# A two-layer AdaLN transformer on one core: the second division of layer 0's heads, two products sooner in VectorE's and GpSimd's order

## The chip, the cores and the metric

The kernel runs on one core of one Trainium2 chip. The metric is the device time of the whole kernel in microseconds (us), the median of three runs. An engine works through its own list of instructions in order; a semaphore wait stops that engine and nothing else. The engines here are TensorE (PE in the profile, its weight loads PEld), VectorE (DVE), ScalarE (ACT), GpSimd (POOL) and SyncE (SP), which issues the DMAs.

## The reference

Two layers work on `x`, 8 batches of 256 tokens of 128 numbers. Each layer adds a gated attention and a gated feed-forward part, and in front of each stands a layer norm that is scaled and shifted by values from `c`. The change touches layer 0's attention alone, whose 16 heads come down to 4 after the mean over groups:

```python
gq = q.reshape(B, G, KV_HEADS, N, D_HEAD)
gk = k.reshape(B, G, KV_HEADS, N, D_HEAD).mean(axis=1)
gv = v.reshape(B, G, KV_HEADS, N, D_HEAD).mean(axis=1)
scores = jnp.einsum('bghnd,bhsd->bhns', gq, gk) + gbias
attn = jax.nn.softmax(scores, axis=-1)
out = jnp.einsum('bhns,bhsd->bhnd', attn, gv)
```

Layer 0's feed-forward part is a mixture of experts per head: for each token and head one of eight experts is chosen, a causal attention follows, and `einsum('bhne,ehkd,bnhk->...')` goes through the chosen output expert. Layer 1 has an attention over the 16 heads of each token and a feed-forward part with eight experts and a capacity. All is float32.

## The kernel before

The kernel is a software pipeline over the eight batches. A function `in_order` writes down one order of work, and each engine runs `in_order` with its own bodies for the pieces (`attn0`, `values`, `front1`, `products`, ...), so that all engines go through the same places. A piece of work of another batch is put beside a loop: the loop calls `beside(place)`, and a dictionary says which steps come at which place. The order of an engine's instructions is therefore written out by hand, and it is not changed at run time.

`products(b, beside)` is layer 0's output experts for one batch: 16 products, numbered by `c`. VectorE makes mask `c + 7` (L1348: the chosen experts, 8-bit, times `oT`, 128 x 512) and then calls `beside(c)`; TensorE waits for mask `c`, does two matmuls (L1853), and then calls `beside(c)`. Seven masks are ahead when the loop starts, so mask 13 is made at place 6, 14 at 7 and 15 at 8.

Beside these products runs the attention of layer 0 for a later batch, `attn0` (dictionary `in_products0`), with the four heads in two pairs. Its steps are:

- QKV: the projections (TensorE L1662, L1666, L1677) and their copies (ScalarE).
- S0, S1: the logits of a pair of heads (TensorE L1693); VectorE adds the bias and takes the greatest (L1233); ScalarE takes the exponentials with their sums (L811).
- N0, N1: the division of a pair. VectorE waits for the pair's exponentials (semaphore `a_e`) and makes the reciprocal of the sums (L1240); GpSimd waits for this (`a_r`) and multiplies the two heads (L650, 128 x 512 each). TensorE and ScalarE have nothing in these steps.
- T0, T1: TensorE waits for each divided head (`a_pn`) and transposes it, four transposes a head (L1709); ScalarE copies the result (L826, L821).
- V0, V1, OUT: the weighting of the values (TensorE L1720) and the copy out (L829).

For the batches 0 and 1, which run ahead in the opening (20 to 40 us), VectorE divides one head of each pair itself (L1246) and GpSimd the other.

In the rounds in the middle the end of layer 1's attention of an earlier batch lies beside the same products (`in_products`). ADD at place 5 adds to `x` and takes the statistics of the layer norm (VectorE L1216, L1201, L1204), from which GpSimd makes `rstd` (L715 adds epsilon, L717 takes the power). NORM at place 7 is VectorE's: it waits for `rstd` and writes `xn`, two instructions L1211. MODULATE at place 9 transposes `xn` on TensorE (L1635, one transpose for each of the two) and applies the modulation on ScalarE (L774). LOGITS at place 11 (TensorE L2033, VectorE L1472) and PROBS at 13 (L1478) follow. The softmax of layer 1's attention (`softmax`) lies there as well: MAXES at place 9 (VectorE L1405, then GpSimd's subtraction L672), EXPS at 12 and SUMS at 14.

Where several plans have steps at one place, the softmax's come first, then `attn0`'s, then those of layer 1's tail. `attn0` of batches 2 to 7 lies beside products of batches 0 to 5; layer 1's tail lies there from the products of batch 2 on, that is in four of the six.

The two engines' bodies of the division:

```python
if n in (N0, N1):                       # VectorE
    p = (N0, N1).index(n)
    dve.wait_ge(s_("a_e"), b * 8 + 4 * p + 4)
    dve.reciprocal(rdenA[:, 4 * p:4 * p + 4], denA[:, 4 * p:4 * p + 4]).then_inc(s_("a_r"), 1)
if n in (N0, N1):                       # GpSimd
    p = (N0, N1).index(n)
    pool.wait_ge(s_("a_r"), b * 2 + p + 1)
    for h in (2 * p, 2 * p + 1)[:1 if early_batch(b) else 2]:
        pool.tensor_tensor(v, v, rdenA[...], ALU.mult).then_inc(s_("a_pn"), 1)
```

Of the kernel before, what the change touches and what calls it, by code (L numbers as in the profile page):

```python
# [44 lines left out]
TAKE, QKV, S0, S1, N0, N1, T0, T1, V0, V1, OUT = range(10, 21)  # L45
# [15 lines left out]
def adaln_kernel(nc, a, out):  # L61
    with ExitStack() as ctx:
# [318 lines left out]
        def in_order(attn0, values, turns, front1, back1, products, masks, opening, last_softmax, after_attn0, after_products,  # L381
# [8 lines left out]
            def alone(place):  # L390
                pass

            in_products0 = {"start": (QKV,), 1: (S0,), 4: (N0, S1), 7: (T0,), 8: (N1,), 11: (T1,), 14: (V0, V1), 15: (OUT,)}
            in_products = {2: (PROJECT,), 5: (ADD,), 7: (NORM,), 9: (MODULATE,), 11: (LOGITS,), 13: (PROBS,)}
            softmax = {"start": (ADDS,), 9: (MAXES,), 12: (EXPS,), 14: (SUMS,)}
            softmax_behind_masks = {6: (ADDS,), 9: (MAXES,), 12: (EXPS,), 14: (SUMS,)}
# [201 lines left out]
        def _(pool):  # L598
# [120 lines left out]
            def after_attn1(b, k, n):  # L719
                after(b, k, n)  # L720
                if n == LOGITS:
                    pool.wait_ge(s_("n_h"), k + 1 + B)
                    pool.tensor_copy(hE[:, bass.ds(b * N, N)], hR[:, :]).then_inc(s_("h_kept"), 1)

            beside = in_order(attn0, values, nothing, front1, back1, products, nothing, opening, last_softmax, after, after,
                              after_front1, after_attn1)
            for b in range(2):
# [5 lines left out]
        def _(act):  # L733
# [246 lines left out]
            def last_softmax(b, beside):  # L980
# [5 lines left out]
                for i in range(2 * T):  # L986
                    keep(0, i)
                beside("probs")

            beside = in_order(attn0, values, turns, front1, back1, products, nothing, opening, last_softmax, after_attn0,  # L990
                              after_products, after_front1, after_attn1)

# [101 lines left out]
        def _(dve):  # L1094
# [368 lines left out]
            def after_attn1(b, k, n):  # L1463
# [10 lines left out]
                if n == PROBS:  # L1474
# [4 lines left out]
                                      lrec[:, :].unsqueeze(2).broadcast_to([P, T, E1]), ALU.mult).then_inc(s_("l_d"), 1)  # L1479

            beside = in_order(attn0, values, turns, front1, back1, products, masks, opening, last_softmax, after_attn0,
                              after_products, after_front1, after_attn1)
            for b in range(2):
# [725 lines left out]
```

## Time and profile before

| | before |
|---|---|
| time, median of 3 runs (lowest to highest) | 759.81 us (759.73 to 759.92) |
| time of the profiled execution | 759.72 us |
| its span, first to last instruction | 757.8 us |
| TensorE busy | 736.5 us (97%) |
| VectorE busy | 553.4 us (73%) |
| ScalarE busy | 384.9 us (51%) |
| GpSimd busy | 187.6 us (25%) |

The share of busy time is a mean over stages. What one wait is worth is read from the stage in which it stands: from the chain of work that ended last, and from the timelines of the engines, which give each instruction's start and duration and the idle time in front of it.

### The profile page before, as it was taken

To read this page: it belongs to the slowest core of one execution; us is meant where nothing else is said; L and a number is where in the kernel's file an instruction comes from. 1 tells how busy PE (TensorE), PEld (TensorE's weight loads), DVE (VectorE), ACT (ScalarE), POOL (GpSimd) and SP (SyncE) were. 2 spreads that over 40 slices of the span, in tenths; PEclk is the share of its full clock that TensorE was granted. 3 is DMA by queue.
4 is the path that set the end of the run, shared out by engine and by line. 5 is a ranking of instruction groups with operands and counts; after the bars stand their busy time and mean duration, and the time that the engine had idled before them with its cause. 6 is when DMAs were issued, how large, how long until landed. Compare 5 with 4: busy or idle time off the path is not lost.

```text
span 757.8 us, 16811 instructions
## 1 busy us (share of the span) xinstructions
PE 736.5 (97%) x6559; PEld 557.8 (74%) x6559; DVE 553.4 (73%) x1642; ACT 384.9 (51%) x1069; POOL 187.6 (25%) x235
## 2 busy tenths in 40 slices
PE   7899999999999999999999999999999899999996
PEld 5566857775786578657865886688578778999996
DVE  4877785868867886778677867787959664255997
ACT  3755657355545654564456445643561446554422
POOL 0232522154015402530254025304210422000000
PEclk9999999999999999999999999999999999999999
DMA  7950020402040204020402130113204304000000
GB/s 209 398 139 1 29 57 2 112 1 57 13 102 2 57 21 93 2 56 19 97 1 56 28 87 15 43 37 78 57 2 113 112 4 110 1 1 1 16 21 22
DMA packets 55702, 43.07 MB, mean 57 GB/s; under 512 B 37900, under 2 KB 48804, under 8 KB 54216
## 3 DMA queue, kind: packets, MB, share of 16 engines
q1 hardware_dynamic: 55624, 42.01, 20.6%
q8 instruction: 52, 0.85, 0.5%
q14 instruction: 26, 0.21, 0.1%
HBM read 32.42 MB, written 9.58 MB: 55 GB/s over the span
## 4 chain that ended last, share of the span: by engine, by line
PE 81%; DVE 12%; POOL 2%; ACT 2%; issue 2%; DMA 1%; SPq 0%; DVEq 0%; ACTq 0%
PE ps L1770 15%; PE ps L1853 11%; PE ps L1913 8%; PE ps L2076 4%; PE ps L2054 4%; PE ps L1756 4%; PE ps L2023 4%; PE ps L1778 4%; PE ps L1865 3%; PE ps L1804 3%; PE ps L1791 3%; DVE shared L1499 2%; DVE shared L1492 2%; PE ps L1936 2%; PE ps L1948 2%; PE ps L1720 2%
## 5 line engine op out<-in xcount | busy, mean ns | idle before, releaser
L1770 PE MATMUL ps<-veF,hB 128*128 128x512 f32 x256 | 121.6, 606 | 0.0
L1318 DVE COPY_PREDICATED shared<-ghot,ps 128x512 f32<-128x512 int32 x128 | 88.3, 727 | 3.4 <-PE ps L1770 0.6
L865 ACT ACTIVATE sc<-sc,nmax 128x128 f32<-128x128 f32 (+1 forms) x128 | 57.2, 448 | 58.4 <-DVE nmax L1304 58.4
L1770 PEld LDWEIGHTS ps<-veF,hB 128*128 128x128 f32 x256 | 45.2, 189 | 49.4 <-issue 40.5
L658 POOL TENSOR_TENSOR sc<-sc,rg 128x384 f32<-128x384 f32 x64 | 51.7, 829 | 69.9 <-DVE rg L1291 69.9
L715 POOL TENSOR_TENSOR ve<-mv,eps 128x2 f32<-128x2 f32 x24 | 8.6, 358 | 230.5 <-DVE mv L1204 230.5
L1853 PE MATMUL ps<-wide,oeF 128*128 128x256 f32 x256 | 62.3, 386 | 0.0
L1913 PE MATMUL ps<-hC,early 128*64 128x128 f32 x1024 | 61.5, 275 | 0.2
L1853 PE MATMUL ps<-early_masks,oeF 128*128 128x256 f32 x256 | 61.3, 382 | 0.0
L2054 PE MATMUL ps<-hE,veF 128*128 128x256 f32 x256 | 59.5, 382 | 0.3 <-ACT wide L974 0.3
L1913 PEld LDWEIGHTS ps<-hC,early 128*64 128x64 f32 x1024 | 55.6, 137 | 5.2 <-issue 3.0
L650 POOL TENSOR_TENSOR sc<-sc,rdenA 128x512 f32<-128x512 f32 x28 | 28.6, 1041 | 112.6 <-DVE rdenA L1240 112.6
L1853 PEld LDWEIGHTS ps<-wide,oeF 128*128 128x128 f32 x256 | 46.7, 190 | 9.7 <-issue 4.3
L1853 PEld LDWEIGHTS ps<-early_masks,oeF 128*128 128x128 f32 x256 | 47.4, 191 | 7.7 <-issue 2.0
L2054 PEld LDWEIGHTS ps<-hE,veF 128*128 128x128 f32 x256 | 47.1, 190 | 7.0 <-ACT wide L974 0.9
L1348 DVE TENSOR_TENSOR early_masks<-chosen,oT 128x512 f32<-128x512 uint8 x64 | 42.1, 684 | 13.6 <-PE ps L1853 12.7
L811 ACT ACTIVATE sc<-sc,nmax 128x256 f32<-128x256 f32 x64 | 31.7, 498 | 31.0 <-DVE nmax L1233 31.0
L1304 DVE CUSTOM_DVE_ANT_0 sc<-ps,causal 128x128 f32<-128x128 f32 (+1 forms) x128 | 40.0, 350 | 9.5 <-PE ps L1778 9.1
L903 ACT ACTIVATE wide<-ps,bqkvT 128x128 f32<-128x128 f32 x128 | 36.1, 374 | 16.1 <-PE ps L1913 16.0
L1348 DVE TENSOR_TENSOR wide<-chosen,oT 128x512 f32<-128x512 uint8 x64 | 42.1, 695 | 0.5 <-PE ps L1853 0.5
L1387 DVE TENSOR_TENSOR early<-ps,early 128x512 f32<-128x512 f32 x32 | 22.1, 689 | 22.4 <-PE ps L1913 22.1
L672 POOL TENSOR_TENSOR wide<-wide,max 128x512 f32<-128x512 f32 x32 | 32.5, 1044 | 22.5 <-DVE max L1405 22.5
(262 smaller groups left out, 1544.2 us busy)
## 6 DMA issues: line engine op xcount, KB each, us to landing
chosen<-hot_scratch SPq DMA_DIRECT2D x16, 512.0 KB, 5.7
v_scratch<-shared SPq DMA_DIRECT2D x16, 512.0 KB, 5.1
vg<-v_scratch SPq DMA_DIRECT2D x16, 512.0 KB, 5.3
veF<-in_L_ffn_value_experts SPq DMA_DIRECT2D x1, 2048.0 KB, 10.2
oeF<-in_L_ffn_output_experts SPq DMA_DIRECT2D x1, 2048.0 KB, 15.3
early<-in_L_attn_w_qkv SPq DMA_DIRECT2D x1, 1536.0 KB, 15.9
shared<-bias_scratch SPq DMA_DIRECT2D x2, 512.0 KB, 4.9
veF<-in_L_ffn_W SPq DMA_DIRECT2D x1, 1024.0 KB, 5.4
```

The source lines that it names most:

```text
L658: pool.tensor_tensor(v, v, rg[:, h, :].unsqueeze(2).broadcast_to([P, 3, P]), ALU.mult).then_inc(s_("f_pn"), 1)
L672: pool.tensor_tensor(quarter(q), quarter(q), max1[:, q, :].unsqueeze(2).broadcast_to([P, PER_ROUND, ROWS]), ALU.subtract).then_inc(s_("c_s ...
L811: act.activation(v, v, ACT.Exp, bias=nmax[:, h, t:t + 1], scale=-1.0, accum_out=denA[:, h * T + t:h * T + t + 1]).then_inc(s_("a_e"), 1)
L865: act.activation(v, v, ACT.Exp, bias=nmax[:, h % RING, t:t + 1], scale=-1.0, accum_out=denB[:, h * T + t:h * T + t + 1]).then_inc(s_("f_e" ...
L903: act.activation(q1[:, :, 2 * j + i, :], ps[:, qk_bank(b, j), i * P:(i + 1) * P].rearrange("p (n t) -> p n t", t=GT), ACT.Identity, bias=b ...
L1304: dve.tensor_tensor_reduce(sc[:, h % RING, lo:hi], ps[:, 4 + 2 * (h % 2), lo:hi], causal[:, P:N] if t == 0 else causal[:, :], -float(DH) * ...
L1318: dve.copy_predicated(val[:, t, :].rearrange("p (h k) -> p h k", h=HF), ghot[:, t * HF:(t + 1) * HF, e].bitcast(I32).unsqueeze(2) .broadca ...
L1348: dve.tensor_tensor(masked(c), chosen[:, c // 4, 2 * (c % 4):2 * (c % 4) + 2, :], oT[:, c // 4, :].unsqueeze(1).broadcast_to([P, 2, N]), A ...
L1770: pe.matmul(ps[:, vbank(j), :], tok(hB, t), veF[:, :].rearrange("p (h e k) -> p e h k", h=HF, e=EF)[:, e, :, :], start=True, stop=True).th ...
L1853: mm = pe.matmul(ps[:, product_bank(b), 0:N], oeF[:, c // 4, (2 * c + j) % 8, :], masked(c)[:, j, :], start=(c == 0 and j == 0), stop=(c = ...
L1913: mm = pe.matmul(ps[c * DH:(c + 1) * DH, qk_bank(b, j), i * P:(i + 1) * P], wqkv1[:, 4 * quad + i, w, :], tok(hC, c), start=True, stop=True)
L2054: mm = pe.matmul(ps[:, hidden_bank(b, e), g * N:(g + 1) * N], w1[:, e, g * P:(g + 1) * P], hE[:, b * N:(b + 1) * N], start=True, stop=True)
```

## The change

One entry of the dictionary `in_products0` moves: N1, the division of heads 2 and 3, stands at place 6 instead of place 8. All else is the same.

```diff
-            in_products0 = {"start": (QKV,), 1: (S0,), 4: (N0, S1), 7: (T0,), 8: (N1,), 11: (T1,), 14: (V0, V1), 15: (OUT,)}
+            in_products0 = {"start": (QKV,), 1: (S0,), 4: (N0, S1), 6: (N1,), 7: (T0,), 11: (T1,), 14: (V0, V1), 15: (OUT,)}
```

## Rows read from the trace of the kernel before

**Rows 1.** The page: its head, and the chain that ended last by engine.

```profile
span 757.8 us, 16811 instructions
...
PE 81%; DVE 12%; POOL 2%; ACT 2%; issue 2%; DMA 1%; SPq 0%; DVEq 0%; ACTq 0%
```

**Rows 2.** Chain of waits, 205 to 246 us: start, us, what.

```profile
227.63 2.05 POOL sc L650 x2
```

**Rows 3.** Timeline of TensorE, same stretch: start, us, instruction, [idle before <- releaser].

```profile
224.10 1.04 PE L1709 MATMUL ps<-ident,sc 128*128 128x128 f32 x8
224.97 1.89 PE L1853 MATMUL ps<-early_masks,oeF 128*128 128x256 f32 x8
226.70 0.55 PE L1635 MATMUL ps<-ident,xn 128*128 128x128 f32 x2
227.09 1.89 PE L1853 MATMUL ps<-early_masks,oeF 128*128 128x256 f32 x8
228.82 0.60 PE L1709 MATMUL ps<-ident,sc 128*128 128x128 f32 x4
229.73 0.66 PE L1709 MATMUL ps<-ident,sc 128*128 128x128 f32 x4 [0.31 <-POOL sc L650]
230.22 0.51 PE L2033 MATMUL ps<-wg,hA 128*128 128x8 f32 x4
```

**Rows 4.** Timeline of VectorE, same stretch.

```profile
224.35 1.26 DVE L1348 TENSOR_TENSOR wide<-chosen,oT 128x512 f32<-128x512 uint8 x2
226.27 0.60 DVE L1211 TENSOR_SCALAR xn<-x,mv,rstd 128x128 f32<-128x128 f32 x2 [0.65 <-issue]
...
227.38 0.17 DVE L1240 RECIPROCAL rdenA<-denA 128x4 f32<-128x4 f32 x1
227.47 2.43 DVE L1405 TENSOR_REDUCE max<-wide 128x8 f32<-128x512 f32 x4
```

**Rows 5.** Timeline of GpSimd, same stretch.

```profile
224.52 0.55 POOL L715 TENSOR_TENSOR ve<-mv,eps 128x2 f32<-128x2 f32 x1 [2.26 <-DVE mv L1204]
225.15 1.03 POOL L717 TENSOR_TENSOR rstd<-ve,half 128x2 f32<-128x2 f32 x1
227.63 2.04 POOL L650 TENSOR_TENSOR sc<-sc,rdenA 128x512 f32<-128x512 f32 x2 [1.46 <-DVE rdenA L1240]
```

**Rows 6.** Who waited for GpSimd's L650, whole span: us in total, times.

```profile
  PE ps L1709: 1.8, 5
```

**Rows 7.** Timeline of ScalarE, same stretch: last sum of head 3.

```profile
223.66 0.19 ACT L811 ACTIVATION_READ_ACCUMULATOR sc<-sc,nmax 128x1 f32 x1
```

**Rows 8.** Timelines of TensorE and GpSimd, products of batch 1 (138 to 172 us).

```profile
154.79 1.04 PE L1709 MATMUL ps<-ident,sc 128*128 128x128 f32 x8
...
152.03 2.04 POOL L650 TENSOR_TENSOR sc<-sc,rdenA 128x512 f32<-128x512 f32 x2 [2.52 <-DVE rdenA L1240]
```

**Rows 9.** L1211, whole span (ns least/median/most); timeline of all engines, 36 to 38.5 us.

```profile
L1211 DVE TENSOR_SCALAR xn<-x,mv,rstd x48: 323/342/998, 36.9 to 652.1; 128x128 f32<-128x128 f32 x48
...
36.12 0.70 POOL L717 TENSOR_TENSOR rstd<-ve,half 128x2 f32<-128x2 f32 x1
36.78 1.04 POOL L650 TENSOR_TENSOR sc<-sc,rdenA 128x512 f32<-128x512 f32 x1
36.91 1.25 DVE L1211 TENSOR_SCALAR xn<-x,mv,rstd 128x128 f32<-128x128 f32 x2 [0.43 <-issue]
```

**Rows 10.** Timelines of VectorE and GpSimd, later in the first stage.

```profile
231.82 0.90 DVE L1478 TENSOR_TENSOR probs<-lexp,lrec 128x16 f32<-128x16 f32 x1
...
229.63 4.05 POOL L672 TENSOR_TENSOR wide<-wide,max 128x512 f32<-128x512 f32 x4
```

**Rows 11.** Stretches: length; busy PE, PEld, DVE, ACT, POOL (instructions); clock, DMA, GB/s.

```profile
230.20:236.20 6.00, 6.00 (x39) 4.49 (x37) 4.29 (x11) 4.06 (x11) 6.00 (x8) 1.00 0.01 3
```

**Rows 12.** Timeline of all engines in the opening, 22 to 25 us.

```profile
22.77 1.50 DVE L1246 TENSOR_SCALAR sc<-sc,rdenA 128x256 f32<-128x256 f32 x2
22.82 1.04 POOL L650 TENSOR_TENSOR sc<-sc,rdenA 128x512 f32<-128x512 f32 x1 [1.48 <-DVE rdenA L1240]
```

## The prediction
> **What bounds the kernel now.** I read the page first, then the chain of waits of one products stage, then the timelines of the engines in that stage. The page says that the chain that ended last runs 81% through TensorE and 12% through VectorE [rows 1]: a wait counts where TensorE stands still for it, and shifts everything behind it.
>
> The edit acts beside the products of six batches, where attn0 of batches 2 to 7 runs. Four of these stages (the rounds that also carry layer 1's tail, 75 us apart) have the same pattern; the rows show the first, from 211 to 236 us. The other two, products of batches 0 and 1, carry no layer norm.
>
> In the stage shown the chain leaves TensorE for the second division, GpSimd's two multiplies L650 [rows 2]. VectorE makes the reciprocal L1240 at 227.38, behind the masks L1348, and behind the layer norm's two L1211, which had stood idle for GpSimd's rstd (L715, L717) [rows 4, 5]. GpSimd then multiplies from 227.63 to 229.67. TensorE turns the two heads at L1709: the first group of four starts at 228.82 on time, the second stands 0.31 until 229.73 [rows 3]. The totals hold 1.8 us for five such waits [rows 6]: four of 0.31, and one in the opening, which the edit leaves alone. So the edit aims at a real wait on the path.
>
> **The change part by part.** Nothing is added or removed: six reciprocals L1240 move forward. On VectorE each passes masks 14 and 15 and, in the four stages, the two L1211. No DMA is moved or passed. GpSimd has no instruction between places 6 and 8, so its list stays the same; only the semaphore a_r, for which its two L650 wait, comes sooner.
>
> *The reciprocal's new place.* It waits for ScalarE's exponentials of heads 2 and 3, whose last accumulator read ends at 223.66 + 0.19 = 223.85 [rows 7]. VectorE reaches place 6 when mask 13, the first of the two at 224.35, is issued: the two last 1.26, so the next instruction starts near 224.95 [rows 4]. No wait is added. The reciprocal takes 0.17, and its successor starts 0.09 behind it (227.38 to 227.47) [rows 4]. Mask 14 thus moves from 224.95 to about 225.03; it is needed only at product 14, after 232, so that is hidden.
>
> *What GpSimd does with it.* Before, its L717 (rstd) ends at 225.15 + 1.03 = 226.18 and GpSimd then stands until 227.63 [rows 5]. After, a_r is there by 225.1, so the first L650 starts as rstd ends. Both multiplies are done some 1.4 us sooner, before TensorE comes for them.
>
> *The gain.* The turn of heads 0 and 1 takes 224.10 to 224.97 = 0.87 until the next TensorE instruction; that of heads 2 and 3 takes 228.82 to 230.22 = 1.40 [rows 3]. Without the wait it takes 0.87 too: 0.53 saved in each of four stages, 2.1 us in all. In the two other stages there is nothing to save: the turn at 154.79 is one block of eight lasting 1.04, as long as the block at 224.10 [rows 3, 8], and the multiplies that it needs end at 152.03 + 2.04 = 154.07 [rows 8].
>
> *The cost.* The time at which GpSimd begins to multiply is also the time at which VectorE wants to normalize. Both are released by the same rstd: before, L1211 starts at 226.27, with GpSimd idle, and the pair takes 0.60 [rows 4]. The opening shows the other case: rstd at 36.12 lasting 0.70, L650 at 36.78 directly behind it, L1211 at 36.91. There the pair takes 1.25 and one of its records 998 ns, where the median is 342 [rows 9]: it ends 0.08 after the multiply (36.91 + 1.00 against 36.78 + 1.04). So this L1211 makes no headway while an L650 runs, and the multiply gets there first. After the change this happens in four stages, with two multiplies in line.
>
> The steps for one stage. Mask 14 lies 0.09 later, and rstd, which was held up by it (1.03 here, 0.70 in the opening [rows 5, 9]), ends at 226.27. The first L650 runs from 226.24 to 227.28. The first L1211 ends 0.08 behind it, at 227.36. The second L650 has been asked for since 227.25, and the second L1211 is issued only as the first ends, so I let the multiply go ahead: it ends at 228.28 and the second L1211 at 228.36. TensorE's transposes of xn (L1635, place 9) need both. Before, the pair ended at 226.87 and the next product started 0.22 later, at 227.09 [rows 3, 4]. After, it starts at 228.36 + 0.22 = 228.58: 1.49 later. If VectorE's first L1211 holds the second multiply up, or if it gets nothing until both multiplies are over, the end is about one step of the pair (0.26) later: 1.75.
>
> That engines take turns between two instructions in a row is shown twice. GpSimd's small L715, issued at 224.52 under mask 13, ends at 225.07, while mask 14 is running [rows 4, 5]. VectorE's L1478 at 231.82 ends at 232.72, while GpSimd's four L672 from 229.63, one each 1.00, run on to 233.68: it ends with the third of them, not with the fourth [rows 10]. So I take 1.49, and keep 1.75 as the upper end.
>
> The Trainium skill, "SBUF — State Buffer", section "Who interferes with whom", says that a `tensor_scalar` in a two-port mode and a GpSimd instruction exclude each other, and that issue order decides who blocks. By that rule the second L1211 stands behind the second multiply, as in my sum; the trace agrees for one pair (998 ns), and no row shows two.
>
> *What is late next.* Mask 15 follows at 228.3, the maxima at 228.9, so GpSimd's subtractions (L672) start near 229.7, as now (229.63) [rows 10]: they gain nothing. TensorE comes to the second turn at about 230.3, when both heads have long been divided: the 0.53 is saved. What follows (logits, the second weighting, the next batch's queries) hangs on TensorE's order and moves with it; TensorE is busy for 6.00 of the 6.00 us up to 236.2 [rows 11], so nothing there absorbs the delay. In the two other stages masks 14 and 15 meet the multiplies and may end up to 2 us later, against a need some 4 us off: nothing.
>
> *The sum.* One stage: +1.49 - 0.53 = +0.96. Four stages: +3.8 (upper end 4 x 1.22 = +4.9). The profiled execution took 759.72, its span 757.8 [rows 1] and 1.9 around it; the median of the runs is 759.81, so 0.1 is added to carry over: 763.7.
>
> **The rivals.**
>
> *The multiplies don't hold the norm up* (ends faster). Then only the gain is left: -2.1, 757.7. For it: the wait at L1709 is on the chain [rows 2, 3]. Against it: the 998 ns [rows 9]. It decides at the point where L1211 is issued before L650; but L650 starts 0.13 ahead in the opening, released by the same event. Chance 0.09.
>
> *Both L1211 slip in behind the first multiply.* Then the pair takes 1.25 as in the opening, from 226.37 to 227.62; the next product starts at 227.84, 0.75 late; less 0.53, that is +0.2 a stage, +0.9, 760.7. Against it: the alternation in [rows 4, 5, 10]. Chance 0.12.
>
> *rstd comes before mask 14.* With the mask started only at 225.03 and L717 at 225.15, GpSimd could get through first and take 0.70: all that follows lies 0.42 earlier, the stall is 1.07, the net 0.54 a stage, +2.2, 762.0. For it: in the opening L650 started 0.05 after VectorE's L1246 and still went first (L1246's pair takes 1.50, its first ends after the multiply) [rows 12]. Against it: here it would be 0.12. Chance 0.13. The Trainium skill's rule on issue order (same page and section) would put the mask first; the rows show that starts 0.05 apart as the trace records them do not obey it.
>
> *No change at all*: GpSimd's list is the same, and the saved wait and the new stall could cancel by some other order of grants. Within 0.2%; chance 0.03.
>
> **How the numbers follow.** The forecast (stall of 1.49 to 1.75 in four stages) has 0.60 and gives 763.7, its own range 763.4 to 765.0. With rstd first 0.13, both norms between the multiplies 0.12, no hold-up 0.09, cancelling 0.03, anything else 0.03. Reaching from 760.5 to 765.0 takes in the first three and leaves out the faster side. A measurement of this kernel can tell 0.2%, 1.5 us, from no change. Slower by more: 0.60 + 0.13 + 0.02 = 0.75. Within: 0.12 + 0.03 = 0.15. Faster: 0.09 + 0.01 = 0.10.
>
> **What would show it.** In the trace of after: L1240 in front of mask 14; L650 directly behind L717 at about 226.2; no standing at L1709; the pair L1211 lasting about 2.0 instead of 0.60; TensorE standing over 1 us at L1635 for xn. If L1211 keeps its 0.60, the forecast is wrong in sign. If the pair takes 1.25, it is wrong in size, through the order of grants. If only L1709's wait moves elsewhere, the path is not what I read.

## The result and the profile after

| | before | after |
|---|---|---|
| time, median of 7 runs (lowest to highest) | 759.17 us (758.03 to 759.92) | 762.32 us (761.36 to 763.09) |
| ratio to before (95% interval) | | 1.0041 (1.0029 to 1.0053) |
| time of the profiled execution | 759.72 us | 762.43 us |
| its span | 757.8 us | 760.5 us |
| VectorE busy | 553.4 us | 560.3 us |

The changed kernel is 3.1 us slower (2.2 to 4.0). The chain that ended last has hardly moved between the engines: compare [rows 1].

```profile
span 760.5 us, 16811 instructions
...
PE 82%; DVE 12%; ACT 2%; DMA 1%; issue 1%; POOL 1%; SPq 0%; DVEq 0%; ACTq 0%
```

The loss is in the four stages. Here is VectorE's timeline of the first, the counterpart of [rows 4]; the stage begins 0.58 later than in the execution before.

```profile
224.93 0.66 DVE L1348 TENSOR_TENSOR wide<-chosen,oT 128x512 f32<-128x512 uint8 x1
225.51 0.17 DVE L1240 RECIPROCAL rdenA<-denA 128x4 f32<-128x4 f32 x1
225.60 0.66 DVE L1348 TENSOR_TENSOR wide<-chosen,oT 128x512 f32<-128x512 uint8 x1
226.91 2.00 DVE L1211 TENSOR_SCALAR xn<-x,mv,rstd 128x128 f32<-128x128 f32 x2 [0.65 <-issue]
228.82 0.68 DVE L1348 TENSOR_TENSOR wide<-chosen,oT 128x512 f32<-128x512 uint8 x1
```

The reciprocal now stands between masks 13 and 14, and nothing waits there. But the norm's two L1211 last 2.00 us instead of 0.60. GpSimd's timeline, the counterpart of [rows 5], shows what lies beside them:

```profile
225.10 0.55 POOL L715 TENSOR_TENSOR ve<-mv,eps 128x2 f32<-128x2 f32 x1 [2.26 <-DVE mv L1204]
225.72 1.09 POOL L717 TENSOR_TENSOR rstd<-ve,half 128x2 f32<-128x2 f32 x1
226.79 2.03 POOL L650 TENSOR_TENSOR sc<-sc,rdenA 128x512 f32<-128x512 f32 x2
230.18 4.04 POOL L672 TENSOR_TENSOR wide<-wide,max 128x512 f32<-128x512 f32 x4 [1.36 <-DVE max L1405]
```

The two multiplies run from 226.79 to 228.82, right behind rstd; the second L1211 ends at 228.91. TensorE's timeline, the counterpart of [rows 3]:

```profile
224.68 1.04 PE L1709 MATMUL ps<-ident,sc 128*128 128x128 f32 x8
225.55 1.89 PE L1853 MATMUL ps<-early_masks,oeF 128*128 128x256 f32 x8
227.96 0.33 PE L1635 MATMUL ps<-ident,xn 128*128 128x128 f32 x1 [0.52 <-DVE xn L1211]
228.96 0.33 PE L1635 MATMUL ps<-ident,xn 128*128 128x128 f32 x1 [0.67 <-DVE xn L1211]
229.12 1.89 PE L1853 MATMUL ps<-early_masks,oeF 128*128 128x256 f32 x8
230.85 1.04 PE L1709 MATMUL ps<-ident,sc 128*128 128x128 f32 x8
231.72 0.51 PE L2033 MATMUL ps<-wg,hA 128*128 128x8 f32 x4
```

The second turn L1709 is one block of eight with no wait: the edit did what it aimed at, 1.40 became 0.87. In its place TensorE stands twice at L1635, for the two tiles of xn. From the first turn to the product behind L1635 it took 2.99 before (224.10 to 227.09) and takes 4.44 now (224.68 to 229.12). From the first turn to the logits L2033 it took 6.12 and takes 7.04. The other three stages agree within 0.01: taken to the nanosecond, +1.456 up to that product and -0.529 from there to the logits, net +0.93 a stage, 3.71 in all four.

The totals of who waited for whom say the same. For L1211, and then for L650, of the kernel after; in [rows 6] five waits stood at L1709, and only the opening's is left (1.4 in this execution, 0.5 in the one before):

```profile
  PE ps L1635: 4.8, 8
...
  PE ps L1709: 1.4, 1
```

The two spans differ by 2.7, not by 3.7. Outside the stages, where both kernels run the same code, the two executions differ too. In the one after the opening ends 0.29 later, TensorE falls 0.29 back at 195 us and gains 0.58 at 344 us, which together come to nothing. What is left is TensorE's clock near 595 us. Busy time by stretches, before and then after:

```profile
590.00:594.00 4.00, 2.27 (x11) 1.66 (x9) 3.62 (x8) 2.61 (x5) 4.00 (x5) 1.00 0.08 22
594.00:598.00 4.00, 3.25 (x29) 2.93 (x30) 1.49 (x5) 0.60 (x1) 2.69 (x3) 0.57 0.98 345
```

```profile
590.00:594.00 4.00, 4.00 (x20) 3.54 (x19) 4.00 (x7) 0.60 (x1) 1.67 (x2) 1.00 0.16 33
594.00:598.00 4.00, 1.96 (x10) 1.37 (x8) 3.58 (x9) 2.29 (x5) 4.00 (x5) 1.00 0.11 29
598.00:606.00 8.00, 7.38 (x154) 6.50 (x156) 5.66 (x16) 4.65 (x11) 3.26 (x5) 1.00 0.70 251
```

In the execution before, TensorE stood for 1.7 of the 4 us up to 594, and the granted clock of the next 4 us was 0.57 on average, between full speed (2.4 GHz) and half of it (1.2 GHz). In the execution after, the same wait comes 3.7 later (2.0 of the 4 us up to 598), and the 8 us behind it were granted 1.00. TensorE's start times, compared instruction by instruction, are 3.7 later after than before at 590 us, and 2.7 later from 602 us on: the lowered clock cost the execution before 1.0. So I compare kernels below by the stage itself: the time from the first turn to the logits, less the 6.12 of before.

### The profile page after: what moved, and what is told of

Same layout as the page of the kernel before. It is cut to its first block, busy times and chain, and to the rows that moved or that the text cites. A ratio compares the mean times of both kernels' runs of the same rounds, so it can differ in the third digit from the quotient of the medians.

```text
span 760.5 us, 16811 instructions
## 1 busy us (share of the span) xinstructions
PE 735.6 (97%) x6559; PEld 557.2 (73%) x6559; DVE 560.3 (74%) x1642; ACT 382.9 (50%) x1069; POOL 189.4 (25%) x235
## 4 chain that ended last, share of the span: by engine, by line
PE 82%; DVE 12%; ACT 2%; DMA 1%; issue 1%; POOL 1%; SPq 0%; DVEq 0%; ACTq 0%
PE ps L1770 15%; PE ps L1853 12%; PE ps L1913 8%; PE ps L2076 4%; PE ps L2054 4%; PE ps L1756 4%; PE ps L2023 4%; PE ps L1778 4%; PE ps L1865 3%; PE ps L1804 3%; PE ps L1791 3%; DVE shared L1499 2%; DVE shared L1492 2%; PE ps L1936 2%; PE ps L1720 2%; PE ps L1948 2%
## 5 line engine op out<-in xcount | busy, mean ns | idle before, releaser
L715 POOL TENSOR_TENSOR ve<-mv,eps 128x2 f32<-128x2 f32 x24 | 8.6, 357 | 229.7 <-DVE mv L1204 229.7
L650 POOL TENSOR_TENSOR sc<-sc,rdenA 128x512 f32<-128x512 f32 x28 | 30.2, 1096 | 105.3 <-DVE rdenA L1240 105.3
L1348 DVE TENSOR_TENSOR wide<-chosen,oT 128x512 f32<-128x512 uint8 x64 | 44.1, 718 | 0.5 <-PE ps L1853 0.5
L672 POOL TENSOR_TENSOR wide<-wide,max 128x512 f32<-128x512 f32 x32 | 32.5, 1042 | 27.9 <-DVE max L1405 27.9
```

The costliest lines, as they stand in the source:

```text
L672: pool.tensor_tensor(quarter(q), quarter(q), max1[:, q, :].unsqueeze(2).broadcast_to([P, PER_ROUND, ROWS]), ALU.subtract).then_inc(s_("c_s ...
L1348: dve.tensor_tensor(masked(c), chosen[:, c // 4, 2 * (c % 4):2 * (c % 4) + 2, :], oT[:, c // 4, :].unsqueeze(1).broadcast_to([P, 2, N]), A ...
```

## The experiments

Theory: the norm's two instructions on VectorE (L1211) make no headway while GpSimd multiplies (L650), and the two engines take turns at the end of each instruction; TensorE then waits for xn. Rival: what costs is the reciprocal's new place among VectorE's own instructions (it pushes masks or the norm). A second rival keeps the contention but not the turns: VectorE waits until GpSimd has nothing left. Lines in the experiments are shifted by up to eleven; the operands tell which instruction is meant. The diffs are excerpts, those of the dictionary against the kernel before; `...` stands for lines left out.

**The multiplies after the norm.** The changed kernel, with a wait on GpSimd in the four stages (`k` is the norm's number, handed down by the round):

```diff
                     pool.wait_ge(s_("a_r"), b * 2 + p + 1)
+                    if p == 1 and k > 0:
+                        pool.wait_ge(s_("n_xn"), k * 2 + TILES + 2)
...
```

> The changed kernel, with one wait more: in the four stages with a layer norm GpSimd's two multiplies L650 wait until VectorE has written xn. VectorE's order is that of the changed kernel. Theory (the norm's two L1211 stand behind GpSimd's multiplies): the pair L1211 goes back to 0.6 us, TensorE doesn't stand at L1635, the multiplies start at or just behind mask 15 (they end 0.2 to 0.6 us sooner than in the kernel before), the wait at the second turn L1709 is gone or under 0.2: 1.4 to 2.1 us faster than before, about 757.4. Rival (what costs is the reciprocal's place among VectorE's instructions): about 3 us slower than before, as in the changed kernel.

Measured: 757.40 us, ratio 0.9978 (0.9967 to 0.9988). VectorE's norm, GpSimd's multiplies and TensorE's second turn:

```profile
226.01 0.60 DVE L1213 TENSOR_SCALAR xn<-x,mv,rstd 128x128 f32<-128x128 f32 x2 [0.65 <-issue]
...
226.76 2.35 POOL L652 TENSOR_TENSOR sc<-sc,rdenA 128x512 f32<-128x512 f32 x2 [0.84 <-DVE xn L1213]
...
228.56 1.26 PE L1711 MATMUL ps<-ident,sc 128*128 128x128 f32 x8
229.66 0.51 PE L2035 MATMUL ps<-wg,hA 128*128 128x8 f32 x4
```

With VectorE's order left as in the changed kernel and only GpSimd's start put behind the norm, the pair is back at 0.60 and the loss is a gain. So the rival of VectorE's order falls. The stage is 0.24 shorter than before, 1.0 in four. That is less than the 1.4 to 2.1 that I expected, though the measured 1.7 lies inside: mask 15 starts first and holds the first multiply up, so the two take 2.35 instead of 2.03, and the second turn takes 1.10, between the 1.40 of before and 0.87. Another 0.06 goes on the way to xn, as mask 14 is still pushed by the reciprocal.

**One multiply more, nothing moved.** The kernel before, with its own order; behind rstd GpSimd multiplies head 0 once more, which nobody reads any longer:

```diff
                 after(b, k, n)
+                if n == ADD and b + 4 < B:
+                    pool.wait_ge(s_("a_pt"), (b + 4) * KV0 + 2)
+                    v = sc[:, 0, :].rearrange("p (t n) -> p t n", t=T)
+                    pool.tensor_tensor(v, v, rdenA[:, 0:T].unsqueeze(2).broadcast_to([P, T, N]), ALU.mult)
```

> The kernel before, with its order of the division; in the four stages one multiply more on GpSimd, 128x512 like L650, stands directly behind rstd (it multiplies head 0's logits, which nobody reads any more). It measures the disputed cost by itself. Theory: the first L1211 stands behind it, the pair lasts 1.25 us, TensorE stands 0.7 at L1635 as with one early multiply, and the wait at L1709 stays at about 0.4: 0.65 a stage, 2.6 us slower than before. Rival (the cost comes from the order of VectorE's instructions): no change, since that order isn't touched.

Measured: 760.80 us, ratio 1.0027 (1.0017 to 1.0038), 2.0 slower.

```profile
225.66 1.04 POOL L724 TENSOR_TENSOR sc<-sc,rdenA 128x512 f32<-128x512 f32 x1
225.78 1.25 DVE L1215 TENSOR_SCALAR xn<-x,mv,rstd 128x128 f32<-128x128 f32 x2 [0.65 <-issue]
...
226.84 0.59 PE L1639 MATMUL ps<-ident,xn 128*128 128x128 f32 x2 [0.46 <-DVE xn L1215]
...
229.90 0.66 PE L1713 MATMUL ps<-ident,sc 128*128 128x128 f32 x4 [0.31 <-POOL sc L650]
```

The reciprocal is where it always was. One multiply alone gives the 1.25 of the opening [rows 9], a stand at L1635, and 0.65 a stage, 2.6 in all, while the old wait at the second turn stays. This is the price of the contention by itself.

**One of the two multiplies early.** The changed kernel's N1 cut by head, head 2 at place 6 and head 3 at place 8. Each step makes the reciprocal of its own two sums and multiplies its own head:

```diff
-4: (N0, S1), 7: (T0,), 8: (N1,), 11: (T1,)
+4: (N0, S1), 6: (N1A,), 7: (T0,), 8: (N1B,), 11: (T1,)
+                if n in (N1A, N1B):                                   # VectorE
+                    h = 2 + (N1A, N1B).index(n)
+                    dve.wait_ge(s_("a_e"), b * 8 + 2 * h + 2)
+                    dve.reciprocal(rdenA[:, 2 * h:2 * h + 2], denA[:, 2 * h:2 * h + 2]).then_inc(s_("a_r"), 1)
...
+                if n in (N1A, N1B):                                   # GpSimd
+                    h = 2 + (N1A, N1B).index(n)
+                    pool.wait_ge(s_("a_r"), 2 * AHEAD + (b - AHEAD) * 3 + h)
...
```

> The division by head: head 2 (reciprocal and multiply) at place 6, head 3 at place 8. One multiply, not two, follows rstd. Theory: only the first L1211 is held up, the pair lasts 1.25 us as in the opening; TensorE stands about 0.7 at L1635, the wait at L1709 (0.53 with what hangs on it) is gone: net 0.2 a stage, about 0.9 us slower than before, 760.1. Rival (VectorE's order costs): as the changed kernel, 3 us slower. Rival (the port is given over only when GpSimd has nothing left): also 1.25, so this run doesn't tell that one apart.

Measured: 760.81 us, ratio 1.0025 (1.0016 to 1.0034), 1.9 slower.

```profile
225.53 1.25 DVE L1218 TENSOR_SCALAR xn<-x,mv,rstd 128x128 f32<-128x128 f32 x2 [0.65 <-issue]
...
226.59 0.58 PE L1646 MATMUL ps<-ident,xn 128*128 128x128 f32 x2 [0.51 <-DVE xn L1218]
...
228.74 1.04 PE L1720 MATMUL ps<-ident,sc 128*128 128x128 f32 x8
```

The pair and the stand are as the theory has them, and the second turn is one block. The stage is 0.18 longer, 0.7 in all. The whole kernel lost more, 1.2 to 2.6. The profiled execution shows where, outside the four stages: TensorE falls back by 0.54 in a block of matmuls at 421 us, which before was one block without a gap, and by 0.37 at a layer norm of a later batch, with no attn0 beside it. There VectorE's norm, before and then here, starts 1.02 instead of 0.65 behind the mask:

```profile
521.37 0.60 DVE L1211 TENSOR_SCALAR xn<-x,mv,rstd 128x128 f32<-128x128 f32 x2 [0.65 <-issue]
```

```profile
421.07 2.40 PE L1924 MATMUL ps<-hC,early 128*64 128x128 f32 x39 [0.26 <-issue]
...
522.15 0.61 DVE L1218 TENSOR_SCALAR xn<-x,mv,rstd 128x128 f32<-128x128 f32 x2 [1.02 <-issue]
```

At "issue" the engine waits for nothing that the profile shows, so the cause of both stays open. The 0.37 shows also in the other kernel that is cut by head, at the end of this section, and in no other; near 421 us three others lose about 0.26. With both the 0.7 comes to 1.6, inside what was measured; whether the other executions lost them too isn't shown.

**The multiplies in halves.** The changed kernel, each multiply in two instructions of 128x256:

```diff
...
+                        if p == 1 and not early_batch(b):
+                            for t in range(T):
+                                v = sc[:, h, t * N:(t + 1) * N]
+                                ins = pool.tensor_tensor(v, v, rdenA[:, h * T + t:h * T + t + 1].broadcast_to([P, N]),
+                                                         ALU.mult)
+                            ins.then_inc(s_("a_pn"), 1)
+                            continue
...
```

> The changed kernel, with each of the two multiplies cut in two halves of 128x256, four instructions in place of two. Theory (the engines take turns at the end of each instruction): each L1211 stands behind one half, some 0.55 us, the pair lasts about 1.2 us in place of 2.0, TensorE stands about 0.6 at L1635; with the 0.53 saved that is 0 to 0.2 a stage, 0 to 0.8 us slower than before. Rival (VectorE waits until GpSimd has nothing left): the pair lasts 2.0 or more, 3 to 4 us slower.

Measured: 759.19 us, ratio 1.0007 (0.9998 to 1.0015).

```profile
225.54 1.14 DVE L1218 TENSOR_SCALAR xn<-x,mv,rstd 128x128 f32<-128x128 f32 x2 [0.65 <-issue]
226.60 1.11 DVE L1355 TENSOR_TENSOR wide<-chosen,oT 128x512 f32<-128x512 uint8 x1
...
225.42 2.77 POOL L652 TENSOR_TENSOR sc<-sc,rdenA 128x256 f32<-128x256 f32 x4
```

The pair ends at 226.68, while GpSimd is only in the third of its four instructions (they end at 228.19). So VectorE does not wait until GpSimd has nothing left: the second rival falls. Each L1211 stands behind one instruction, and the shorter that is, the less it costs: 0.07 a stage instead of 0.93. The mask behind them (1.11 instead of 0.66 to 0.69) stands behind the third, and the fourth behind the mask.

**One product sooner, in front of the norm.**

```diff
-7: (T0,), 8: (N1,)
+7: (T0, N1)
```

> The division moved by one product only, to place 7 in front of the layer norm; on VectorE the reciprocal passes mask 15 and the norm, not mask 14. Theory: what counts is which side of the norm it lies on, so the pair L1211 lasts 2.0 us as in the changed kernel and the time is the same, 2.7 to 3.3 us slower than before; rstd is 0.1 sooner as mask 14 isn't pushed. Rival (the cost goes with the distance, or comes from mask 14 and rstd): about half of that or less, 0 to 1.5 us slower.

Measured: 761.91 us, ratio 1.0041 (1.0028 to 1.0055).

```profile
225.93 2.00 DVE L1211 TENSOR_SCALAR xn<-x,mv,rstd 128x128 f32<-128x128 f32 x2 [0.56 <-issue]
```

Half the distance, the same loss: 0.86 a stage, 3.5 in all. The 0.06 less than in the changed kernel is rstd: L717 takes 1.02 here and 1.09 there, as mask 14 is not pushed.

**One product sooner, behind the norm.** The same place 7, but as a plan of its own after that of layer 1's tail, so that VectorE's reciprocal follows L1211:

```diff
-7: (T0,), 8: (N1,)
+7: (T0,)
...
+                if not last:
+                    more.append((attn0, b + 3, 0, {7: (N1,)}))
                 products(b + 1, beside((after_front1, b, 0, softmax), *more))
...
```

> The division one product sooner, at place 7, but behind the layer norm: on VectorE the reciprocal passes mask 15 alone. Theory: the norm keeps its 0.6 us; the first multiply now meets mask 15, which starts first and takes 0.5 us, so the multiplies end 0.2 to 0.3 us sooner than before: a gain of 0.2 to 0.3 a stage, 0.8 to 1.2 us faster than before. Rival (any earlier place of the reciprocal costs on VectorE): slower than before.

Measured: 757.75 us, ratio 0.9987 (0.9978 to 0.9996), 1.0 faster.

```profile
226.29 0.60 DVE L1213 TENSOR_SCALAR xn<-x,mv,rstd 128x128 f32<-128x128 f32 x2 [0.65 <-issue]
226.81 0.17 DVE L1242 RECIPROCAL rdenA<-denA 128x4 f32<-128x4 f32 x1
...
227.06 2.40 POOL L652 TENSOR_TENSOR sc<-sc,rdenA 128x512 f32<-128x512 f32 x2 [0.86 <-DVE rdenA L1242]
```

The same place in the dictionary, on the other side of the norm: 4 us apart. The stage is 0.25 shorter, 1.0 in four.

**The stages without a norm.** N1 at place 6 beside the products of batches 0 and 1 alone:

```diff
+            in_products0_free = {"start": (QKV,), 1: (S0,), 4: (N0, S1), 6: (N1,), 7: (T0,), 11: (T1,), 14: (V0, V1), 15: (OUT,)}
-                more = [] if last else [(attn0, b + 3, 0, in_products0)]
+                more = [] if last else [(attn0, b + 3, 0, in_products0_free if first else in_products0)]
...
```

> The division at place 6 beside the products of batches 0 and 1 alone, the two stages without a layer norm; at place 8 in the other four. Theory: nothing in these stages waits for the division, and the masks that meet the multiplies are early enough: no change, within 0.3 us in the stages. Rival (masks 14 and 15 held up by the multiplies cost something): slower by up to 1 us in two stages.

Measured: 759.13 us, ratio 1.0002 (0.9993 to 1.0010).

```profile
83.61 2.10 DVE L1349 TENSOR_TENSOR wide<-chosen,oT 128x512 f32<-128x512 uint8 x2
...
83.76 2.85 POOL L651 TENSOR_TENSOR sc<-sc,rdenA 128x512 f32<-128x512 f32 x2 [1.31 <-DVE rdenA L1241]
...
87.17 1.04 PE L1710 MATMUL ps<-ident,sc 128*128 128x128 f32 x8
```

Masks 14 and 15 meet the multiplies too, and take 2.10 instead of 1.28. Nobody waits for them, and the turn is one block as before: through both stages TensorE's start times keep the same distance to those of the kernel before. No change.

**A version that beats both.** N1 cut by head as above, but head 2 at place 5, in front of the statistics, where GpSimd stands idle; head 3 stays at place 8:

```diff
-4: (N0, S1), 7: (T0,), 8: (N1,), 11: (T1,)
+4: (N0, S1), 5: (N1A,), 7: (T0,), 8: (N1B,), 11: (T1,)
```

> The division by head: head 2 at place 5, in front of the statistics, where GpSimd stands idle and rstd isn't yet asked for; head 3 at place 8 as before. Theory: no multiply follows rstd, the pair L1211 keeps 0.6 us, head 3 is ready 1 us sooner than before, the wait at the second turn is gone: 1.7 to 2.1 us faster than before, about 757.2. Rival (the wait at L1709 is hidden by another, so removing it gives nothing): no change from before. Rival (head 2's multiply pushes mask 13 and rstd): within 0.5 us of before.

Measured: 757.38 us, ratio 0.9979 (0.9969 to 0.9988), 1.6 faster than before and some 5 us faster than the changed kernel.

```profile
222.58 1.04 POOL L650 TENSOR_TENSOR sc<-sc,rdenA 128x512 f32<-128x512 f32 x1 [1.26 <-DVE rdenA L1247]
...
226.77 1.04 POOL L650 TENSOR_TENSOR sc<-sc,rdenA 128x512 f32<-128x512 f32 x1 [1.45 <-DVE rdenA L1247]
...
225.41 0.60 DVE L1218 TENSOR_SCALAR xn<-x,mv,rstd 128x128 f32<-128x128 f32 x2 [0.65 <-issue]
...
227.97 1.04 PE L1720 MATMUL ps<-ident,sc 128*128 128x128 f32 x8
```

One multiply lies in front of rstd and one behind the norm, none between; the pair keeps its 0.60 and the turn is one block. The whole 0.53 of the second turn is saved, 0.10 is given back on the way to xn: 0.43 a stage, 1.7 in all.

All runs in one table. The stage is TensorE's time from the first turn to the logits, less that of the kernel before, in the four stages with a norm; the last column is worked out from the ratio and its interval.

| kernel | pair L1211, us | one stage, us | four stages, us | measured against before, us |
|---|---|---|---|---|
| changed kernel | 2.00 | +0.93 | +3.7 | +3.1 (2.2 to 4.0) |
| multiplies after the norm | 0.60 | -0.24 | -1.0 | -1.7 (-2.5 to -0.9) |
| one multiply more, nothing moved | 1.25 | +0.65 | +2.6 | +2.0 (1.3 to 2.9) |
| one multiply early | 1.25 | +0.18 | +0.7 | +1.9 (1.2 to 2.6) |
| multiplies in halves | 1.14 | +0.07 | +0.3 | +0.5 (-0.2 to 1.1) |
| place 7, in front of the norm | 2.00 | +0.86 | +3.5 | +3.1 (2.1 to 4.2) |
| place 7, behind the norm | 0.60 | -0.25 | -1.0 | -1.0 (-1.7 to -0.3) |
| stages without a norm | 0.60 | 0.00 | 0.0 | +0.2 (-0.5 to 0.8) |
| by head, places 5 and 8 | 0.60 | -0.43 | -1.7 | -1.6 (-2.4 to -0.9) |

## Why the prediction was right

- *The reciprocal waits for nothing at its new place.* Right: it starts at 225.51, as soon as mask 13 is issued.
- *The gain at the second turn, 0.53 a stage.* Right: 1.40 became 0.87 in all four.
- *GpSimd's multiplies start as rstd ends, 0.13 ahead of the norm, and hold it up.* Right: L650 at 226.79, L1211 at 226.91, 0.12 ahead. That this is the cost is shown by the kernel in which nothing moves and one multiply is added, and by the one in which only the multiplies go behind the norm; what is left to the reciprocal's place is the pushed mask 14, some 0.06 a stage.
- *The second multiply goes between the two L1211.* Right, and shown by the halves: VectorE gets in at the end of each GpSimd instruction. The norms' pair ends 0.08 behind the second multiply, as in the sum. With it fall the rivals in which the pair takes 1.25 or 0.60. My upper end, 1.75, needed the first L1211 to hold the second multiply up, or both to wait for both; neither shows: the multiplies take 2.03, as alone.
- *The stall, 1.49.* It is 1.46. The small difference lies in rstd: from the start of L715 to the end of L717 it took 1.66 before and takes 1.72 now, 0.06 more; I had put 0.09 there for the pushed mask. It did not get in front of mask 14 (L717 starts at 225.72, the mask at 225.60), so that rival falls.
- *What is late next.* The subtractions L672 start 5.53 behind the first turn before, 5.50 after: they gained nothing, as said. The two stages without a norm are unchanged, as said.
- *The sum.* Predicted +3.8, in the stages +3.7, measured +3.1 with 2.2 to 4.0. The predicted 763.7 is 1.4 above the 762.32: 0.6 of that is the time before, whose median over seven runs is 759.17 and was 759.81 over the first three. The rest is inside the interval, and outside the stages, where single executions differ by more than that. The measured time lies below the forecast's own range, 763.4 to 765.0, and inside the stated 760.5 to 765.0, which was drawn so wide to take in two rivals. By the time alone, the rival with rstd first (762.0) would have fitted better; that the forecast holds and the rival doesn't is read from the stages.

What stays open is why, in the run with one early multiply, engines stand outside the stages: its stages say +0.7 and the measured time at least +1.2.

## What to carry to other kernels

An engine that stands idle beside the critical path may still be in the way: before a step is moved to where its own engine is free, look at which instruction of the neighbour is released by the same event, because that is the one it will run beside. Where the two contend, put the long instruction wholly in front of or behind the short one that somebody waits for, or cut it. And a wait on the chain of 0.5 us is not worth 0.5 us until it is known what the earlier work will collide with.

## What the runs showed of the hardware

VectorE's L1211 (128x128, float32 from SBUF to SBUF) doesn't get through while GpSimd's multiply (128x512, 1.04 us) runs, and gets in at the end of each such instruction: with one multiply the pair takes 1.25, with two 2.00, with four halves of 0.6 it takes 1.14. Taken to the nanosecond, an L1211 that stands behind a multiply or a half ends 0.08 behind it in all these runs. The multiplies lose nothing by it here: 2.03 for two beside the norm, 2.04 without. The masks (two SBUF inputs) and the multiplies hold each other up: two masks take 2.10 beside the multiplies and 1.28 without, and two multiplies 2.85 beside these masks. VectorE's reductions L1405 keep their time: four take 2.43 beside L650 in the kernel before, and 2.45 in the changed one, where L650 is over. What I had not expected is how regular the turns are: in the halves' run norm, norm, mask and the GpSimd instructions alternate one by one. The Trainium skill, "SBUF — State Buffer", section "Who interferes with whom", has the exclusion and that it lasts a whole instruction, with which these runs agree; whose turn it is when both have work waiting, they show beyond it.
